# Second expert product of a routed feed-forward in three float32r products instead of one float32 product

## The reference

```
probs = softmax(x @ router_w.T);  topk_vals, topk_idx = top_k(probs, 2)
for eid in range(8):
    w = sum(where(idx == eid, vals, 0))
    h = gelu(x_flat @ w1[eid].T)          # exact gelu
    y = h @ w2[eid].T
    out = out + w[:, None] * y
x = layernorm(x + out)
```

## Time and profile before

| | |
|---|---|
| median of 3 runs | 821.5 us (818.32 to 822.62) |
| the profiled execution's own time | 821.51 us |
| its span, first to last instruction | 819.7 us |
| mean granted TensorE clock | 0.931 of 2.4 GHz |
| TensorE busy | 726.1 us (89%) |
| VectorE, ScalarE, GpSimd busy | 334.0, 287.5, 223.1 us |

### The profile page before, as it was taken

One profiled execution on the slowest core, in us unless ns is written; L12 is line 12 of the kernel. 1 busy time (PEld: TensorE's weight loads), 2 busy tenths in 40 slices (PEclk: granted clock), 3 DMA queues, 4 the chain that ended last, 5 costly groups with the idle time before them and its releaser, 6 DMA issues.

```text
span 819.7 us, 11598 instructions
## 1 busy us (share of the span) xinstructions
PE 726.1 (89%) x3964; PEld 469.8 (57%) x3965; DVE 334.0 (41%) x762; ACT 287.5 (35%) x525; POOL 223.1 (27%) x280
## 2 busy tenths in 40 slices
PE   6899999999999689997977947989999999999970
PEld 3323233322224365554555436969999999999960
DVE  3687777689982654533536151300000000000004
ACT  2246656667764433434332312111111111111112
POOL 2211111111115421102041341543333333333322
PEclk9869999999999989999987667989999999999995
DMA  5974124424432160001020077666666665566616
GB/s 160 182 168 93 17 66 91 79 61 96 79 115 81 49 208 1 1 1 51 1 52 0 7 200 238 170 134 165 173 182 185 190 169 164 157 179 180 171 11 205
DMA packets 58910, 92.84 MB, mean 113 GB/s; under 512 B 13841, under 2 KB 45298, under 8 KB 57331
## 3 DMA queue, kind: packets, MB, share of 16 engines
q1 hardware_dynamic: 50355, 83.86, 36.5%
q0 software_dynamic: 8512, 8.44, 6.6%
HBM read 75.94 MB, written 17.86 MB: 114 GB/s over the span
## 4 chain that ended last, share of the span: by engine, by line
PE 77%; DVE 8%; DMA 5%; ACT 4%; issue 3%; POOL 2%; SPq 1%; POOLq 0%; DVEq 0%; ACTq 0%
PE ps L1888 16%; PE ps L1899 16%; PE ps L1568 7%; PE ps L1559 7%; PE ps L1493 6%; PE ps L1597 3%; DVE nmx L1061 2%; PE ps L1511 2%; PE ps L1724 2%; PE ps L1683 2%; ACT probs L859 2%; PE ps L1714 2%; PE ps L1580 1%; PE ps L1717 1%; PE ps L1672 1%
## 5 line engine op out<-in xcount | busy, mean ns | idle before, releaser
L859 ACT ACTIVATE probs<-ps 128x512 f32<-128x512 f32 x256 | 136.0, 604 | 102.7 <-PE ps L1559 102.1
L1061 DVE TENSOR_REDUCE nmx<-ps 128x1 f32<-128x512 f32 x256 | 159.7, 680 | 15.7 <-PE ps L1493 15.0
L1888 PEld LDWEIGHTS ps<-xtT,w1c 128*128 128x128 f32 x1248 | 146.2, 193 | 2.4 <-issue 0.5
L1888 PE MATMUL ps<-xtT,w1c 128*128 128x128 f32 x1248 | 146.8, 276 | 0.4 <-issue 0.4
L1899 PE MATMUL ps<-wexp,hidT 128*128 x624 | 144.0, 385 | 0.7 <-issue 0.7
L1899 PEld LDWEIGHTS ps<-wexp,hidT 128*128 128x128 f32 x624 | 117.7, 194 | 16.3 <-issue 1.6
L1454 DVE TENSOR_SCALAR yw<-ps,mt 128x256 f32<-128x256 f32 x39 | 18.9, 484 | 256.3 <-PE ps L1899 254.1
L1022 ACT ACTIVATE hidT<-ps 128x1024 f32<-128x1024 f32 x39 | 39.9, 1023 | 225.8 <-PE ps L1888 207.2
L804 POOL DMA_INDIRECT acc<-yw,mt x39 | 62.0, 1589 | 170.7 <-DVE yw L1454 163.9
L1493 PE MATMUL ps<-kst,qst 96*128 96x512 bf16 x256 | 98.7, 409 | 4.5 <-DVE nmx L1061 3.1
L1559 PE MATMUL ps<-qst,kst 99*128 99x512 bf16 x256 | 94.0, 391 | 1.0 <-ACT probs L859 0.7
(11 more groups left out here) (204 smaller groups left out, 780.8 us busy)
## 6 DMA issues: line engine op xcount, KB each, us to landing
w1c<-in_w1T SPq DMA_DIRECT2D x39, 1024.0 KB
wexp<-in_w2T SPq DMA_DIRECT2D x8, 1024.0 KB
kst<-scrk SPq DMA_DIRECT2D x48, 128.0 KB, 6.9
qst<-scrq SPq DMA_DIRECT2D x8, 384.0 KB, 4.8
xTb<-in_xT SPq DMA_DIRECT2D x4, 512.0 KB, 7.6
qst<-scrq SPq DMA_DIRECT2D x8, 256.0 KB, 5.4
xr<-in_x SPq DMA_DIRECT2D x4, 512.0 KB, 5.1
x2d<-xr SPq DMA_DIRECT2D x4, 512.0 KB, 4.0
```

What stands on the lines that cost most here:

```text
L859: act.activation(probs[n % 8][:, :], ps[:, 4 + n % 3, :], ACT.Exp).then_inc(s_exp, 1)
L1061: dve.tensor_reduce(nmx[w % 2][:, k:k + 1], ps[:, ring_bank("max", w, k), :], AX.X, ALU.max, negate=True).then_inc(s_mfree, 1)
L1888: mm = pe.matmul(ps[:, 2 * (j % 2) + f // 4, f % 4 * P:(f % 4 + 1) * P], w1c[j % 2][:, k * FF + f * P:k * FF + (f + 1) * P], xtT[j % 2][:, ...
```

## The change

expert_out no longer multiplies float32 numbers. The gelu result and the slot's w2 are each split into a high part (the number rounded to float32r) and a low part (the rest, also float32r), and the product is high by w_high, plus high by w_low, plus low by w_high: 24 products of 256 columns per slot in place of 8 float32 ones. The product of the two low parts is left out. ScalarE makes the high parts (`gelu_high`, 128 x 1024; `w2_high`, 128 x 2048, reading the slot's expert from the plan), VectorE the low parts (`gelu_low`, `w2_low`), slot by slot, in two buffers of each. `gelu_high`, `w2_high` and `gelu_low` of slot t wait for expert_out(t-2), which frees their buffers. ScalarE's order becomes gelu(t+1), copy_xtT(t+2), gelu_high(t+1), w2_high(t+2); VectorE's weigh(t), w2_low(t+2), gelu_low(t+2). At the head of the stage w2_high(0) stands before gelu(0) on ScalarE, and w2_low(0), gelu_low(0) before slots(3) on VectorE.

```diff
+    w2h = [sb(f"w2h{i}", EW, F32R, R_K) for i in range(2)]
+    w2l = [sb(f"w2l{i}", EW, F32R, R_K) for i in range(2)]
+    hidh = [sb(f"hidh{i}", FF, F32R, R_P) for i in range(2)]
+    hidl = [sb(f"hidl{i}", FF, F32R, R_P) for i in range(2)]
...
@@ ScalarE
         def gelu(t, j):
             act.wait_ge(s_mm1, t + 1)
             if not (isinstance(t, int) and t < 2):
+                act.wait_ge(s_hl, t - 1)
+            act.activation(hidT[j % 2][:, :], bank(2 * (j % 2), 2), ACT.Gelu).then_inc(s_h, 1)
+
+        def gelu_high(t, j):
+            act.wait_ge(s_h, t + 1)
+            if not (isinstance(t, int) and t < 2):
                 act.wait_ge(s_mm2, t - 1)
-            act.activation(hidT[j % 2][:, :], bank(2 * (j % 2), 2), ACT.Gelu).then_inc(s_h, 1)
-
+            act.activation(hidh[j % 2][:, :], hidT[j % 2][:, :], ACT.Copy).then_inc(s_hh, 1)
+
+        def w2_high(t, j):
+            e = act.value_load(plan[0][0:1, ds(t, 1)], min_val=0, max_val=NE - 1)
+            if not (isinstance(t, int) and t < 2):
+                act.wait_ge(s_mm2, t - 1)
+            act.activation(w2h[j % 2][:, :], wexp[:, ds(e * EW, EW)], ACT.Copy).then_inc(s_wh, 1)
+
+        act.wait_ge(s_planned, 1)
+        act.wait_ge(s_we, 16 * NE)
+        w2_high(0, 0)
         gelu(0, 0)
-        with act.Fori(0, NSLOT // 4) as i:
+        gelu_high(0, 0)
+        w2_high(1, 1)
+
+        def slot_front(t, j):
+            last = isinstance(t, int)
+            if not (last and t + 1 >= NSLOT):
+                gelu(t + 1, j + 1)
+            if not (last and t + 2 >= NSLOT):
+                copy_xtT(t + 2, j + 2)
+            if not (last and t + 1 >= NSLOT):
+                gelu_high(t + 1, j + 1)
+            if not (last and t + 2 >= NSLOT):
+                w2_high(t + 2, j + 2)
+
+        for t in range(4):
+            slot_front(t, t)
...
@@ VectorE
         second_choice(3)
-        slots(3)
...
+        def gelu_low(t):
+            dve.wait_ge(s_hh, t + 1)
+            if t >= 2:
+                dve.wait_ge(s_mm2, t - 1)
+            dve.tensor_tensor(hidl[t % 2][:, :], hidT[t % 2][:, :], hidh[t % 2][:, :], ALU.subtract).then_inc(s_hl, 1)
+
+        def w2_low(t):
+            e = dve.value_load(plan[0][0:1, t:t + 1], min_val=0, max_val=NE - 1)
+            dve.wait_ge(s_wh, t + 1)
+            dve.tensor_tensor(w2l[t % 2][:, :], wexp[:, ds(e * EW, EW)], w2h[t % 2][:, :], ALU.subtract).then_inc(s_wl, 1)
+
+        dve.wait_ge(s_planned, 1)
+        w2_low(0)
+        gelu_low(0)
+        slots(3)
+        w2_low(1)
+        gelu_low(1)
         for group, (lo, hi) in enumerate(META_GROUPS):
             dve.wait_ge(s_mt[group], 16 * (hi - lo))
             for t in range(lo, hi):
                 weigh(t)
+                if t + 2 < NSLOT:
+                    w2_low(t + 2)
+                    gelu_low(t + 2)
                 if t == 1:
                     plan_rest()
...
@@ TensorE
         def expert_out(t, j):
-            e = pe.value_load(plan[0][0:1, ds(t, 1)], min_val=0, max_val=NE - 1)
-            pe.wait_ge(s_h, t + 1)
             if not (isinstance(t, int) and t < 2):
                 pe.wait_ge(s_yw, t - 1)
+            pe.wait_ge(s_hl, t + 1)
+            pe.wait_ge(s_wl, t + 1)
             for f in range(KF):
-                mm = pe.matmul(ps[:, 4 + j % 2, 0:D], hidT[j % 2][:, f * P:(f + 1) * P],
-                               wexp[:, ds(e * EW + f * D, D)], start=(f == 0), stop=(f == KF - 1))
+                high, low = (of[j % 2][:, f * P:(f + 1) * P] for of in (hidh, hidl))
+                w_high, w_low = (of[j % 2][:, f * D:(f + 1) * D] for of in (w2h, w2l))
+                pe.matmul(ps[:, 4 + j % 2, 0:D], high, w_high, start=(f == 0), stop=False)
+                pe.matmul(ps[:, 4 + j % 2, 0:D], high, w_low, start=False, stop=False)
+                mm = pe.matmul(ps[:, 4 + j % 2, 0:D], low, w_high, start=False, stop=(f == KF - 1))
             mm.then_inc(s_mm2, 1)
```

More of the change, by code:

```diff
@@ L224, in at_expert @@
         return sb(name, cols, dt, R_Q + 8 * KB * e, rows)
+    EW = KF * D
     KW = NB * HB * SC
@@ L240, in decoder_layer @@
     k2tl = at_expert(4, "k2tl", KD * NB * SC, F32R)
+    place[R_K], place[R_P] = R_K, R_P
+    w2h = [sb(f"w2h{i}", EW, F32R, R_K) for i in range(2)]
+    w2l = [sb(f"w2l{i}", EW, F32R, R_K) for i in range(2)]
+    assert place[R_K] <= LATE
+    hidh = [sb(f"hidh{i}", FF, F32R, R_P) for i in range(2)]
+    hidl = [sb(f"hidl{i}", FF, F32R, R_P) for i in range(2)]
+    assert place[R_P] <= R_END
     place[R_P] = R_P
@@ L264, in decoder_layer @@
     assert place[Y_REG] <= R_K + 64 * KB
-    EW = KF * D
     place[R_Q] = R_Q
@@ L357, in decoder_layer @@
     s_h = sem("gelu_ready")
+    s_hh = sem("gelu_high_ready")
+    s_hl = sem("gelu_low_ready")
+    s_wh = sem("w2_high_ready")
+    s_wl = sem("w2_low_ready")
     s_w1c = [sem(f"w1_loaded_{k}") for k in range(2)]
@@ L1020, in gelu @@
             if not (isinstance(t, int) and t < 2):
-                act.wait_ge(s_mm2, t - 1)
-            act.activation(hidT[j % 2][:, :], bank(2 * (j % 2), 2), ACT.Gelu).then_inc(s_h, 1)
-        gelu(0, 0)
-        with act.Fori(0, NSLOT // 4) as i:
-            for j in range(4):
-                gelu(4 * i + j + 1, j + 1)
-                copy_xtT(4 * i + j + 2, j + 2)
+                act.wait_ge(s_hl, t - 1)
[3 more added lines that the diff above has]
+            if not (isinstance(t, int) and t < 2):
+                act.wait_ge(s_mm2, t - 1)
+            act.activation(hidh[j % 2][:, :], hidT[j % 2][:, :], ACT.Copy).then_inc(s_hh, 1)
[7 more added lines that the diff above has]
+        w2_high(0, 0)
+        gelu(0, 0)
+        gelu_high(0, 0)
[12 more added lines that the diff above has]
+            slot_front(t, t)
+        with act.Fori(1, EARLY // 4 - 1) as i:
+            for j in range(4):
+                slot_front(4 * i + j, j)
+        act.wait_ge(s_planned, 2)
+        with act.Fori(EARLY // 4 - 1, NSLOT // 4) as i:
+            for j in range(4):
+                slot_front(4 * i + j, j)
         for t in range(NSLOT // 4 * 4, NSLOT):
[L1030 to L1033, removed]
+            slot_front(t, t)
         for n in range(NT - QT):
@@ L1459, in _ @@
                 weigh(t)
+                if t + 2 < NSLOT:
+                    w2_low(t + 2)
+                    gelu_low(t + 2)
                 if t == 1:
                     plan_rest()
+                if t + 2 == EARLY - 1:
+                    dve.wait_ge(s_planned, 2)
         for b in range(NB):
@@ L1922, in _ @@
         pe.wait_ge(s_xTs, 2 * len(E_ORDER))
-        pe.wait_ge(s_we, 16 * NE)
         expert_out(0, 0)
@@ L1930, in _ @@
             tile(j, j, 0)
[L1931 to L1935, removed]
+        with pe.Fori(1, NSLOT // 4) as i:
             for j in range(4):
```

## The result

The changed kernel takes 816.8 us in the median (813.8 to 820.0, 14 runs) against 821.9 (813.3 to 826.6, 14 runs): ratio 0.9947, 95% interval 0.9923 to 0.9970. It is 0.5% faster, under half of the 1.2% that was forecast. The profiled execution took 813.9 us, its span is 812.1.

What follows compares the result with a forecast made beforehand. TensorE was taken to bound the steady slot (7.25 us). Span 819.7 + 8.7 (head) - 18.6 (32 slots x 0.58) = 809.8 us, with 1.8 outside it 811.6, 1.2% less; range 802 to 824.

Steps and rivals of the forecast that it cites:

- The product: expert_out: 24 float32r products at 0.12 us, 2.88 us per slot against 3.46, saving 0.58 in each of 32 slots.
- Rival 4: expert_out: load and stream don't overlap, 0.22 us per product, near 896; or no shrinking with columns, 907; chance 0.07.
- The head: Start of the expert stage: nothing hides the splits; at turn_tile(7) the kernel is 8.7 us behind.
- some tenths: Splits in the steady slot: what the plan's value loads were said to add, in us.
- the second, 4.7 at turn_tile(6): Head: TensorE waits some 4.7 us ahead of turn_tile(6), to 553, because gather(6) is issued late.
- plan_rest didn't hold scatter(2): Head: plan_rest, 4.7 us, comes late on VectorE, to 539.9; weigh(2) stands behind it, so scatter(2) waits until 541.15.
- The half clock behind the idle stretches: Head: TensorE runs at 1.2 GHz after idle time; behind the turn_tile(6) wait this costs 3.4 us.
- All split work costs nothing in the steady slot: Steady slot of 6.67 us: ScalarE's 4.36 us and VectorE's 3.96 fit, so the splits cost nothing.
- sees its scatter at the same place: Steady slot: weigh slips 0.5 us against the turn, as much as the product gains, so GpSimd's scatter keeps its place.
- rival 5: Steady slot: VectorE's two-SBUF-input subtractions hold up GpSimd's gathers and scatters by 2.3 us each, 859; chance 0.10, part only eating the gain.
- the first case: Whole kernel: the forecast itself; the products gain, the head gives half back; 811.6 us; chance 0.55.
- the second: Whole kernel: worse head (13 us) or dearer product (0.1225 to 0.128 us), ending within 0.5%, at 818; chance 0.19.

Runs made afterwards that it cites:

- e2: Kernel before with the 24 float32r products but no splits (gelu writes the high part, other parts constants): 799.3 us, 0.9758 of the kernel before.
- e6: Changed kernel with w2_high and w2_low of slots 0 and 1 moved ahead of the last batch's router work: 811.9 us, 0.9854 of the kernel before.
- h4: Kernel before with gathers issued a slot earlier and the routing scatters spread two per slot: 814.6 us, 0.9909 of the kernel before.
- h2: h1 with the eight routing scatters issued two behind each of scatters 1 to 4, not four behind 1 and 2: 803.8 us, 0.9759.
- g1: Changed kernel with w2_low on 8 of its 2048 columns from slot 8: 814.0 us, 0.9901 of the kernel before.
- e4: Changed kernel with GpSimd issuing gather(t+4) where it issued gather(t+3): 807.8 us, 0.9812 of the kernel before.
- h1: Changed kernel with the edits of e4 and e6 together: 805.2 us, 0.9787 of the kernel before.
- e1: Changed kernel with all its splits but the float32 product of before, the parts unused: 837.6 us, 1.0200 of the kernel before.
- f1: Kernel before with two extra 128 x 2048 VectorE subtractions per slot from slot 8, both inputs in SBUF, result unused: 827.8 us.
- f2: Kernel before with two extra 128 x 2048 VectorE subtractions per slot from slot 8, one input in PSUM, result unused: 822.0 us.

## Why the prediction was half right

**The product: right.** 0.12 us apart, 2.87 us a slot (forecast 2.88), a slot of 6.66 us (6.67). Each product has a weight load of its own, and loads alone need 0.111 us: they lie under the running product. Rival 4, that they don't overlap or that the product doesn't shrink, is refuted. The rule of the Trainium skill ("TensorE: Matmul & The Clock Gate", Part 3) that a load overlaps only where the row group differs doesn't hold in these rows.

**The head: right in kind, mis-sized.** The term was 8.7 us, and it measured 11.5. Forecast and measured, each counted from its trace's hidden(0) (the forecast's times less 500.05):

| us after hidden(0) | forecast | measured | late by |
|---|---|---|---|
| weigh(0) | 24.95 | 27.83 | 2.9 |
| scatter(0) | 25.75 | 29.12 | 3.4 |
| gather(4) | 27.65 | 32.33 | 4.7 |
| scatter(1) | 29.85 | 35.09 | 5.2 |
| gather(5) | 36.85 | 43.31 | 6.5 |
| turn_tile(5) | 41.45 | 50.41 | 9.0 |
| turn_tile(6) | 52.95 | 59.73 | 6.8 |
| turn_tile(7) | 63.60 | 66.40 | 2.8 |

Of the first 2.9 us, 1.56 lie ahead of any split: hidden(1) starts 7.94 us after hidden(0), 6.38 before. In e2 it is 6.48, in e6 6.64 and in h4 7.59, so it comes and goes with the execution, and the forecast couldn't have it; and 0.95 is TensorE's idle time, 5.05 instead of 4.1 us. The chain shows 0.75 us of VectorE's value load (DVEq L1504) ahead of w2_low(0), which I had as "some tenths". Then comes the step that failed: "scatter(1) goes at 529.9, gather(5) 7.0 us later ... at 536.9, landing about 541.5 ... a wait of 2.5 us". scatter(0) took 2.90 us beside w2_low(2) (525.03), not 1.6; scatter(1) had to wait for its landing, 5.12 us after its start; scatter(1), beside w2_low(3), and the first L771, beside gelu_low(3), took 1.2 us more than in the trace of before; and gather(5) needed 7.06 us to its turn where I took 4.6. Of that last term 1.6 us stood in my own rows: the same gather(5) of before goes at 530.32 and is turned at 536.49, 6.17 us later. That GpSimd's scatters keep their length beside the splits, and that a gather lands in 4.6 us, are what the head's term had wrong. The one wait was 8.3 us, and the second, 4.7 at turn_tile(6), didn't come: at turn_tile(6) TensorE was by then late itself. plan_rest didn't hold scatter(2), GpSimd's own queue did; that step came true in h2, with the other waits gone. The half clock behind the idle stretches was as forecast. Why gather(5) took 7.06 us to land isn't settled; the DMA share was 0.79 in that wait. Nor was GpSimd's hold-up at the head run by itself: that it makes part of the head's loss is read from these rows.

**The steady slot: the step "All split work costs nothing in the steady slot" fell.** 31 slots should have saved 31 x 0.58 = 18.0 us and saved 15.14: 2.9 us missing. VectorE and ScalarE did have the room: e4 and h1 do all the split work in a steady piece of 206.47 us, with no wait in it. What was wrong is that GpSimd "sees its scatter at the same place" and its gathers stay at 1.06: w2_low makes 2.5 of the 2.9 us, by g1. The forecast had this as rival 5 and gave its partial form no price.

**The sum.** 2.8 + 2.9 less 0.1 at the end is 5.6 us, which is the forecast's 9.9 less the 4.35 measured. Up to 1.6 of the head's 2.8 us are chance, the slow hidden(0) of this one execution; the waits for gathers are not, as g1 and e4 show. The result lies on the line between the first case and the second. The fifth, by which the kernel would have been slower, is right in mechanism and wrong in size: of a slot's two indirect DMAs only the gather stands beside w2_low (the scatters' median stayed at 1.59), so GpSimd never became the bound.

## What to carry to other kernels

A product that gets cheaper by work on other engines should be priced twice: in the steady loop, where that work hides, and at the loop's head, where it stands in line ahead of the first product (here 16.5 us in e1, against the 22.5 that e2 gained in head and steady piece). When the bound engine gets faster, look for what was just in time: here issuing the gathers one place earlier gave back 9 us. And check each long VectorE instruction with two SBUF inputs against what GpSimd issues beside it.

## Of the hardware

GpSimd's issue of an indirect DMA is held up by a VectorE instruction with two inputs in SBUF: gathers 1.06 to 1.9 or 2.2 us, scatters 1.59 to 2.9 or 3.7; with one input in PSUM not at all (f1, f2). Whether a second input or the amount read from SBUF decides isn't separated. The Trainium skill ("SBUF — State Buffer", Who interferes with whom) states that contention for a GpSimd instruction that reads SBUF; the runs agree in that they show it for the issue of these DMAs; that the issue reads SBUF no run shows.

A float32r product of 128 x 128 on 256 columns takes 0.12 us in a row at full clock, its weight load included, and 0.21 us at half clock; so at full clock it is not quite twice as fast.
